# Spreading the reciprocal degrees of layer 0 with two DMAs instead of TensorE products and a ScalarE copy

## The reference

```python
def hypergraph_conv(x, adj, W, b):
    H = (adj != 0).astype(x.dtype)
    w = adj.reshape(N, -1)[:, :C]                 # first row of adj
    xw = jnp.einsum('ncd,hd->nch', x, W)
    Dn = jnp.einsum('nce,ne->nc', H, w)
    Dn = jnp.where(Dn > 0, 1.0 / Dn, 0.0)         # reciprocal degrees
    Be = H.sum(axis=1)
    Be = jnp.where(Be > 0, 1.0 / Be, 0.0)
    m = Be[:, :, None] * jnp.einsum('nce,nch->neh', H, xw)
    out = Dn[:, :, None] * jnp.einsum('nce,neh->nch', H, m)
    return out + b
h = jax.nn.relu(hypergraph_conv(x, adj, W1, b1))
h = layer_norm(h, gamma, beta)
y = hypergraph_conv(h, adj, W2, b2) + x
x = _layernorm(x + y)
```

## Time and profile before

| | us |
|---|---|
| median of 3 runs (lowest, highest) | 670.11 (669.84, 670.38) |
| profiled execution | 670.04 |
| its span, first to last instruction | 668.2 |
| TensorE busy | 623.1 (93%) |
| VectorE busy | 560.8 (84%) |
| ScalarE busy | 526.6 (79%) |
| GpSimd busy | 376.5 (56%) |
| chain that ended last, share of TensorE | 30% |

### The profile page before, as it was taken

One profiled execution on the slowest core, in us unless ns is written; L12 is line 12 of the kernel. 1 busy time (PEld: TensorE's weight loads), 2 busy tenths in 40 slices (PEclk: granted clock), 3 DMA queues, 4 the chain that ended last, 5 costly groups with the idle time before them and its releaser, 6 DMA issues.

```text
span 668.2 us, 15857 instructions
## 1 busy us (share of the span) xinstructions
PE 623.1 (93%) x5014; PEld 452.0 (68%) x5014; DVE 560.8 (84%) x1712; ACT 526.6 (79%) x1191; POOL 376.5 (56%) x448
## 2 busy tenths in 40 slices
PE   5989999999999999898999979999999997999993
PEld 4667777777777776565666646666666664778882
DVE  3889998888888888778999888988988987688886
ACT  4667888877777777868999788787877785899995
POOL 1234556665555557756777435353535353899983
PEclk9999999999999999998999999999999998999998
DMA  9591338354646433344655334545453443487773
GB/s 271 182 233 48 80 65 221 79 145 82 149 87 150 86 65 63 63 81 89 103 110 98 63 75 85 111 81 109 83 110 83 103 87 64 81 188 188 180 188 127
DMA packets 174466, 76.14 MB, mean 114 GB/s; under 512 B 122160, under 2 KB 173872, under 8 KB 174384
## 3 DMA queue, kind: packets, MB, share of 16 engines
q1 hardware_dynamic: 164208, 66.34, 42.3%
q0 software_dynamic: 8448, 8.39, 8.5%
q10 hardware_dynamic: 1728, 0.40, 0.3%
HBM read 28.97 MB, written 8.39 MB: 56 GB/s over the span
## 4 chain that ended last, share of the span: by engine, by line
PE 30%; DVE 8%; POOL 6%; DMA 6%; ACT 3%; issue 2%; SPq 0%; ACTq 0%; POOLq 0%; DVEq 0%
PE banks L86 9%; PE banks L88 8%; PE banks L87 8%; DMA xT_lo<-x_halves 3%; DMA l_TT_lo<-l_T_lo 3%; DVE l_st L1057 2%; POOL x_halves L1143 2%; POOL l_rstd L1082 2%; PE banks L1237 2%; POOL l_U L2048 1%; PE banks L1605 1%; POOL l_T_lo L1845 1%; ACT l_t L1658 1%; DVE l_u L1762 1%; DVE l_rsum L1768 1%
## 5 line engine op out<-in xcount | busy, mean ns | idle before, releaser
L1091 ACT ACTIVATE x_resident<-l_pre,l_nmr,l_rstd 128x256 f32<-128x256 f32 x256 | 140.8, 605 | 7.7 <-POOL l_nmr L1085 7.7
L983 POOL TENSOR_TENSOR hq<-hq 128x512 f32<-128x512 f32 x48 | 71.7, 1493 | 90.9 <-ACT hq L690 88.6
L1143 POOL TENSOR_TENSOR x_halves<-x_resident,x_halves 128x1024 f16<-128x1024 f32 x46 | 98.1, 2133 | 16.5 <-DVE l_pre L1339 9.9
L1057 DVE BATCH_NORM_STATS2 l_st<-l_pre 128x6 f32<-128x256 f32 x256 | 93.3, 410 | 0.0
L86 PE MATMUL banks<-Wk_lo,xT_hi 128*128 128x512 f16 (+1 forms) x256 | 83.4, 326 | 3.3 <-DVE l_pre L1339 1.8
L87 PE MATMUL banks<-Wk_hi,xT_lo 128*128 128x512 f16 (+1 forms) x256 | 83.3, 325 | 0.0
L88 PE MATMUL banks<-Wk_hi,xT_hi 128*128 128x512 f16 (+1 forms) x256 | 83.2, 325 | 0.0
L1082 POOL TENSOR_TENSOR l_rstd<-l_veps,minus_half 128x4 f32<-128x4 f32 x64 | 71.7, 1121 | 15.1 <-DVE l_veps L1071 11.2
L86 PE MATMUL banks<-W2T_lo,h_hi 128*128 128x257 f16 x256 | 70.2, 274 | 3.5 <-DVE h_lo L849 1.3
L88 PE MATMUL banks<-W2T_hi,h_hi 128*128 128x257 f16 x256 | 70.1, 274 | 0.0
L87 PE MATMUL banks<-W2T_hi,h_lo 128*128 128x257 f16 x256 | 70.1, 274 | 0.0
(11 more groups left out here) (200 smaller groups left out, 1904.8 us busy)
## 6 DMA issues: line engine op xcount, KB each, us to landing
adj<-in_adj SPq DMA_DIRECT2D x32, 256.0 KB, 3.5
x_halves<-in_x SPq DMA_DIRECT2D x16, 512.0 KB, 4.3
x_resident<-b_half SPq DMA_DIRECT2D x8, 1024.0 KB, 7.9
x_resident<-in_x POOLq DMA_DIRECT2D x16, 512.0 KB, 5.9
out<-x_resident SPq DMA_DIRECT2D x15, 512.0 KB, 3.2
x_resident<-in_L_gnn_W SPq DMA_DIRECT2D x2, 512.0 KB, 5.5
x_resident<-in_L_gnn_Wk SPq DMA_DIRECT2D x1, 768.0 KB, 9.6
xT_hi<-x_halves SPq DMA_TRANSPOSE x48, 3.2
```

The costliest lines, as they stand in the source:

```text
L983: pool.tensor_tensor(hq[:, 0, :], hq[:, 0, :], hq[:, h, :], ALU.add).then_inc(hqs_ok, 1)
L1057: dve.bn_stats(L.st[p][:, j, :], L.pre[p][:, j, :]).then_inc(L.st_ok, 1)
L1091: act.activation(K.x[:, gcols(g, j)], L.pre[p][:, j, :], ACT.Identity, bias=L.nmr[p][:, j:j + 1], scale=L.rstd[p][:, j:j + 1]).then_inc(L. ...
L1143: pool.tensor_tensor(F.xs[p][1], x_group(K, g), F.xs[p][0], ALU.subtract).then_inc(F.x_lo, 1)
```

## The change

A small array `degree_rows` in memory, [16, 128, 4], is added. For groups 2 to 15 SyncE's new `spread_degrees(g)`, ahead of `load(g+2)` in its step, waits for `dchain`, writes `dinv` to the group's row of the array, waits for that to land and for P of the group before, and reads the row back, 512 values to each of 128 partitions, into `dbc`. The values now lie with the node outside and the graph inside, so `operator` reads `dbc` with a step of four elements (16 bytes), and it waits for `dbc_in`. TensorE's products, ScalarE's copy and VectorE's two halves are only done for groups 0 and 1. `transpose_adj(g)` waits for `dchain` (the reads of bank 0) of the group before instead of the copy, and layer 1's first product likewise.

```diff
--- before.py
+++ after.py
@@ -124,6 +124,7 @@
         K.xd = x.rearrange("g n d -> n g d")
         K.ad = adj.rearrange("g n e -> n g e")
         K.od = out.rearrange("g n d -> n g d")
+        K.rows = nc.dram_tensor("degree_rows", (G, N, GP), F32)
 
         K.adjn = [sb(f"adj{p}", [128, GP, N]) for p in range(2)]
         K.adj_in, K.x_in, K.xst_in = ([ctx.enter_context(nc.semaphore(f"{name}{p}")) for p in range(2)]
@@ -473,8 +474,8 @@
     adj_in, x_in, xst, xst_in = K.adj_in, K.x_in, K.xst, K.xst_in
     adjT_ps, adjT_sb, inc_ok, wcol_ok, small, incb_ok = map(
         sem, ("adjT_ps", "adjT_sb", "inc_ok", "wcol_ok", "small", "incb_ok"))
-    deg_ps, gram_ps, dinv_ok, dbc_ps, dbc_sb, pf_ok = map(
-        sem, ("deg_ps", "gram_ps", "dinv_ok", "dbc_ps", "dbc_sb", "pf_ok"))
+    deg_ps, gram_ps, dinv_ok, dbc_ps, dbc_sb, pf_ok, row_out, dbc_in = map(
+        sem, ("deg_ps", "gram_ps", "dinv_ok", "dbc_ps", "dbc_sb", "pf_ok", "row_out", "dbc_in"))
     px_ps, px_hi, px_lo = map(sem, ("px_ps", "px_hi", "px_lo"))
     hid_ps, hf_ok, h_hi, h_sq, h_lo, hqs_ok = map(
         sem, ("hid_ps", "hf_ok", "h_hi", "h_sq", "h_lo", "hqs_ok"))
@@ -484,7 +485,7 @@
     y_ps = sem("y_ps")
     dchain = sem("dchain")
     K.hid_read = h_hi, hf_ok
-    K.first_x, K.first_free = L.x_new, dict(adj=adjT_ps, inc=gram_ps, degree=deg_ps, spread=dbc_sb, operator=pf_ok,
+    K.first_x, K.first_free = L.x_new, dict(adj=adjT_ps, inc=gram_ps, degree=deg_ps, spread=dchain, operator=pf_ok,
                                             relu=(h_hi, hf_ok), z=zf_ok, zvar=zvar_ok, squares=sq_lo, wk=W.wk_lo, out=L.pre_ok, copied=adjT_sb)
 
     def sync(sp):
@@ -507,6 +508,14 @@
             if STAGED - 2 < g < G - 1 and g % 2:
                 fill_x(K, sp, (g + 1) // 2)
 
+        def spread_degrees(g):
+            sp.wait_ge(dchain, upto(g, 4, 4))
+            sp.dma_start(K.rows[g], dinv[:]).then_inc(row_out, 16)
+            sp.wait_ge(row_out, 16 * (g - 1))
+            sp.wait_ge(pf_ok, upto(g - 1, 1, 1))
+            sp.dma_start(dbc[:], K.rows[g:g + 1].rearrange("a n j -> a (n j)").to_broadcast([128, C])).then_inc(
+                dbc_in, 16)
+
         def first_halves(g):
             for i in range(2):
                 sp.wait_ge((K.F.x_hi, K.F.x_lo)[i], g + 1)
@@ -517,6 +526,8 @@
         def step(g, p, has):
             if is_first(g):
                 W.sync(sp)
+            if has(0) and g >= 2:
+                spread_degrees(g)
             if has(2):
                 load(g + 2, p)
             if g >= G:
@@ -528,7 +539,9 @@
             if is_first(g):
                 pe.wait_ge(W.const, 7)
             pe.wait_ge(adj_in[p], 8 * (g - p) + 16)
-            if reused(g, 1):
+            if g > 2:
+                pe.wait_ge(dchain, upto(g - 1, 4, 2))
+            elif g > 0:
                 pe.wait_ge(dbc_sb, upto(g - 1, 1, 1))
             for j in range(GP):
                 m = pe.transpose(b_adj[:, j * N:(j + 1) * N], adjn[p][:, j, :], K.ident[:])
@@ -633,7 +646,7 @@
             q = 1 - p
             if has(-1):
                 hidden(g - 1, q, 0)
-            if has(0):
+            if has(0) and g < 2:
                 spread_degrees(g, p)
             if has(-1):
                 hidden(g - 1, q, 1)
@@ -755,7 +768,7 @@
                 hidden(g, 1)
                 square(g, 0)
             once(g, -1, W.high_w1, act)
-            if has(1):
+            if has(1) and g < 1:
                 copy_degrees(g + 1)
             if has(0):
                 hidden(g, 2)
@@ -833,7 +846,11 @@
             dve.wait_ge(dchain, upto(g, 4, 2))
             dve.reciprocal(drc[:], dcl[:]).then_inc(dchain, 1)
             dve.wait_ge(dchain, upto(g, 4, 3))
+            if g > 2:
+                dve.wait_ge(row_out, 16 * (g - 2))
             dve.tensor_tensor(dinv[:], drc[:], dpos[:], ALU.mult).then_inc(dchain, 1)
+            if g > 1:
+                return
             dve.wait_ge(dchain, upto(g, 4, 4))
             if reused(g, 1):
                 dve.wait_ge(dbc_ps, upto(g - 1, 1, 1))
@@ -851,9 +868,14 @@
 
         def operator(g, p):
             dve.wait_ge(gram_ps, upto(g, 1, 1))
+            if reused(g):
+                dve.wait_ge(dbc_in, 16 * (g - 1))
+                dve.wait_ge(y_ps, upto(g - 2, 2, 2))
+                dve.tensor_tensor(pf[p][:].rearrange("p (j n) -> p j n", j=GP),
+                                  b_gram[:].rearrange("p (j n) -> p j n", j=GP),
+                                  dbc[:].rearrange("p (n j) -> p j n", j=GP), ALU.mult).then_inc(pf_ok, 1)
+                return
             dve.wait_ge(dbc_sb, upto(g, 1, 1))
-            if reused(g):
-                dve.wait_ge(y_ps, upto(g - 2, 2, 2))
             dve.tensor_tensor(pf[p][:], b_gram[:], dbc[:], ALU.mult).then_inc(pf_ok, 1)
 
         def mixed_low(g, p, d):
@@ -1209,7 +1231,7 @@
             elif reused(g, 1):
                 pe.wait_ge(qkv_sb, upto(g - 1, GP, j + 1))
             elif j < 2:
-                pe.wait_ge((free["spread"], free["operator"])[j], G)
+                pe.wait_ge((free["spread"], free["operator"])[j], (4 * G, G)[j])
             else:
                 for read in free["relu"]:
                     pe.wait_ge(read, upto(G - 1, HT, j + 1))
```

## The result

The changed kernel takes 681.57 us (median of 4 runs, 678.88 to 682.37), the kernel before, run beside it, 670.25 us (median of 4). The ratio is 1.0154, 95% interval 1.0116 to 1.0193: slower, by 10 to 11 us. The profiled execution took 680.88 us, its span is 679.1 us, 10.9 more than before.

What follows compares the result with a forecast made beforehand. TensorE was taken as the bound, 15.8 us of a 16.08 us late step, with one chain beside it. Start of step 6 +15.2, steps 6 to 15 −8.1: +7.1 on 670.11, so 677.2 us, range 671 to 684.

Steps and rivals of the forecast that it cites:

- signs of being wrong: dbc's DMA of group 5 landing before 108, late steps staying at 15.6 us or more, or P's rows well over 0.7.
- The stall of step 5: SyncE's spread_degrees(5) stands behind the wait for W.done and a fill, so mix_x(5, 0) starts 13.7 us late.
- stall at a fill in later steps: Broadcast 0.4 us late behind a 1 MB fill, taken by VectorE's idle time: 0, at worst 1 us in each of four steps.
- Step 2: Row write behind two fills, broadcast lands at 53.6; VectorE is 3.0 us late and the next step starts 3.0 later.
- Steps 3 and 4: Ordinary steps ahead of step 5, gaining 0.75 and 0.95 us, so step 5 starts 1.3 us late.
- The DMA prices: Row write to memory 1.7 us, broadcast of 256 KB 3.5, together 5.2 us: hidden in the 8.1 us before operator.
- rival B: SyncE's queue does not serve in order, the row write overtakes fills: 669.3 us, or 667.5 with a faster broadcast; chance 0.13.
- The half clock: TensorE at half clock for some 3.4 us behind the long stall: 1.7 us more, ends 0 and 3.4.
- The strided read: VectorE's operator reads dbc in steps of 16 bytes: bounded between 0.68 and 1.36 us, taken as 0.68.
- rival A: The strided read costs: operator at 1.36 us, steps 2 to 5 each 0.68 longer, 679.9 to 684 us; chance 0.18.
- the gain of a late step: Products and copy gone, hole before the last project closes: 16.08 to 15.33 us, 0.75 gained, 1.05 in two steps.
- rival C: No stall, and the fills cost nothing: 14 steps gain 0.75 to 1.05 us, about 12 us less, 658; chance 0.03.

Runs made afterwards that it cites:

- Moving the wait: Changed kernel with SyncE's wait for W.done and the fill of group pair 3 issued after spread_degrees(5), not before it: 674.7 us, ratio 1.0074.
- the kernel with the fills behind: Changed kernel with every fill that followed a load, and the wait for W.done, issued later, behind a spread_degrees: 664.76 us, ratio 0.9922.
- the two edits that had to be made together: On the kernel with the fills behind: GpSimd's add_x put behind the third sum, and transpose_adj(g+1) ahead of hidden(g-1, 2): 665.06 us, ratio 0.9909.

## Why the prediction came out as it did

The direction was right, and 681.57 us lies in the range of 671 to 684, 4.4 us above the forecast (by the profiled spans, 3.8: +10.9 where the sum has +7.1). Two of the prediction's own signs of being wrong came true all the same: late steps stayed over 15.6 us, and P's rows were well over 0.7. Step by step:

- *The stall of step 5* is the mechanism named, nearly at its times: the fill at 104.74 (I had 104.8), the broadcast issued at 109.91 (111.2), P started at 113.88 (114.7), `mix_x(5, 0)` at 115.03 (115.4). Step 6 starts at 121.34 instead of 106.8: +14.5, where the sum has +15.2. Moving the wait showed that this stall goes with it. What I had not seen is that the next one, in step 6, waits behind: the prediction had no stall at a fill in later steps, and as it stands there is none, because step 5's own stall gives the queue 13 us to drain (waits of 0.21 and 0.17 us at fills later on, where I had 0.4).
- *Step 2*: P(2) at 52.98 (I had 53.6), the next step at 59.88 instead of 58.12: +1.8, where I had +3.0. P came 2.35 us late and took 0.38 longer, but "the next step starts 3.0 later" does not follow from that: from P to the next step it was 6.90 us instead of 7.49, as fewer of VectorE's rows for the weights stand there.
- *Steps 3 and 4* gained 0.51 and 0.45 us, where the working has 0.75 and 0.95. Step 5 so started 0.8 us late (I had 1.3), since step 2 had lost less.
- *The DMA prices* were good: the broadcast 3.8 us (3.5 taken), the row write, where nothing stands ahead, 1.4 (1.7 taken; up to 2.9 in other steps without a fill). That the queue serves in order holds at the fills, where the row write landed just behind the last one: rival B, and with it a time below 670, needed the opposite.
- *The half clock*: 1.4 us measured, 1.7 taken.
- *The strided read* was the open term. I took 0.68 us; it is 1.09, 1.6 times the contiguous one and below the 1.36 of rival A. The penalty that the Trainium skill states (Advanced Engine Details and Errata, Memory Cachelines) is there: by that rule, the trace agrees, with +0.41 us for this shape. VectorE's idle time in late steps hides it, so rival A was right in the operation and nearly without effect in the time. That the median lies also in A's range (679.9 to 684) is luck: the strided read is in the kernel with the fills behind, too, and that is faster than the one before.
- *The mis-sized term is the gain of a late step.* I had 0.75 us (1.05 with `Wk_lo`), and it is 0.45 in both kinds. The step of the working that failed is "The chain moves up by 0.45 + 0.5 = 0.95, TensorE by 0.45, so the hole of 0.3 closes", and with it 15.33. It missed two things. It put at nothing a wait of TensorE: the eight products had covered the time in which ScalarE reads the bank of `hidden(g-1, 2)`, and without them 0.22 us of it stand open; this alone holds a step at 15.57. And the chain's upper part did move by 0.92 (the first sum's start), but 0.48 of that was taken back by the sum itself, 1.80 us instead of 1.32 in its new place; the chain, moved by only 0.45, alone holds a step at 15.63. So the hole before `project` closed, and a new one of nearly its size opened. With that, everything from step 6 on brings −3.6 instead of −8.1, and 14.5 − 3.6 = 10.9 is the difference of the spans.

The smaller gain is 4.5 us of the miss, and the two stalls, together 0.7 us cheaper up to step 6 than forecast, take some of it back. One sum of the prediction is off by itself: fourteen steps with 0.75 to 1.05 give 11.1 us, so rival C is 659 and not 658. That it takes both the wait for the bank and the chain to explain the 15.63 is shown by the two edits that had to be made together for 15.34. That the longer sum comes from VectorE's `h_lo` beside it is argued: its length follows the overlap in every trace here, both work on SBUF alone, and beside P, with an input in PSUM, the second sum keeps 1.33 us. No run took `h_lo` away from it.

## What to carry to other kernels

A small DMA whose result an engine needs at once must not be put behind bulk transfers, or behind a wait made for one, on the same queue: list what is issued ahead of it in every step, and put the bulk behind it. Taking one stall away shows the next one in the same queue, so follow the queue for a few steps. And when two nearly equal paths run through a step, taking work off both gives only what the slower one gives back in its new place: re-read each duration there, for it can grow by its new neighbours, and ask what wait of its own engine the removed work had covered.

## What the runs showed of the hardware

- VectorE, fp32 128x512 from a PSUM and an SBUF input: 0.68 us contiguous, 1.09 with the SBUF input in steps of 16 bytes.
- ScalarE, copy of 128x512 fp32 from PSUM: 0.59 us contiguous, 1.11 when it writes in steps of 16 bytes.
- A 2 KB write of 128 pieces of 16 bytes lands 1.4 us after its issue when alone. Issued within 1.1 us of a fill of 1 MB in steps 2 and 5 of the changed kernel, it landed 8.8 and 4.5 us after its issue began, 0.4 and 0.2 us behind the fill, and its issue held SyncE for 2.95 and 0.66 us. With two fills in the 4.1 us ahead of it the issue took 2.29 to 3.01 us in four of the traces; it took 0.85 in the one where the first of two fills was 4.8 us ahead.
- GpSimd's first sum of two 128x512 fp32 tiles took 1.31 to 1.33 us where VectorE's `h_lo` (two inputs in SBUF) ran beside 0.2 to 0.3 us of its first 1.3, and 1.70 to 1.82 where it was 0.6 to 0.7. The second sum, behind the issue of a DMA on GpSimd, took 1.78 us, and 1.33 with this issue moved away.
- After a rest of 12.62 us TensorE was granted 0.50, and 1.00 again from 118 us on, 3 us after it had started; it cost 1.4 us. Kept busy, it stayed at 1.00.
